# Attention and dense experts in one block: slots written out, rows split, turned and routed tile by tile, first dense products among attention's last steps

## The chip, the cores and the metric

The kernel runs on one core of a Trainium2 chip. The metric is the device time of one execution in microseconds (us); the median of several runs counts. The core has TensorE (PE, matmuls and transposes), VectorE (DVE), ScalarE (ACT), GpSimd (POOL) and SyncE (SP, which issues most of the transfers). Each engine works through its own instructions in order and waits on semaphores for the others.

## What is computed

The input x has 2048 rows of 256 numbers (16 tiles of 128 rows). Two layers follow each other, each with a residual: an attention with fp8-rounded projections, half of it over the rows themselves and half over a second input `ctx`, and a feed-forward layer with a shared (dense) expert and a choice of 2 out of 8 experts for each row. Cut to its core:

```python
x = x + xattn(layernorm(x), ctx)          # q, k, v, qx by fp8-rounded products; kx, vx from ctx; wproj
h = layernorm(x)
logits = h @ router_w
top_logits, top_indices = top_k(logits, 2);  scores = softmax(top_logits)
combined = sum over the 2 experts e chosen: score * ((silu(h @ w1[e][:, :512]) * (h @ w1[e][:, 512:])) @ w2[e])
shared = (silu(h @ w_gate) * (h @ w_up)) @ w_down          # 1024 wide
x = x + combined + shared
```

## The kernel before

**Three blocks of instructions.** The program has three blocks, one after the other, and at a block's end all engines wait for each other: attention; the dense expert with the routing; the eight experts. The change is about the first two.

**Attention.** Its work is cut into 64 units: for each of the 16 tiles i four units r (0 and 1 over the rows themselves, 2 and 3 over ctx). `run_slots` lays the steps of the units out in slots: in slot N every engine does one step each of several units, and the number beside a step says how far ahead of N its unit is. On TensorE a slot holds, in this order, the scores of unit N+1 (`pe_scores`), the first transposes of N+2, project 0 of N+3, the turn of the probabilities of N (`pe_probT`), project 1 of N+3, the second transposes of N+2 (`pe_transpose(1)`), the values of N-1 (`pe_values`), project 2 of N+3, the third transposes of N+2, the output product of N-2 (`pe_out`) and project 3 of N+3. VectorE's slot begins with the maximum of the scores of N+1 (`mx`) and the first scaling `nrm` of N+2, which the second transposes read. Slots -3 to 7 and 44 to 66 are written out; slots 8 to 43 are a loop (`Fori`) over tiles, with the tile's number in a register. ScalarE also squares the 30 pieces of the feed-forward weights (`act_weight_squares`, one in every second slot), whose sums give the scales by which the weights are split into two fp16 halves.

**Dense block.** Before its first product it must have the sums of all 30 pieces, six small steps on VectorE that turn them into scales (`scales_end`), the layer norm of the rows (`rstd3`, `normalise`), each row split into two fp16 numbers (`rows_high` on ScalarE, `rows_low` on VectorE), transposed in pairs of tiles (`turn`), evicted (`turned`) and multiplied by the router's weights (`route`), and the pieces 0 to 3 of the dense weights loaded and split (`shared`). Then 32 slots follow (`run_slots3`): 4 groups of 512 rows by 8 slices of 128 of the 1024 columns. In slot N TensorE does `up` of N+1, which is a gate product and an up product of 6 matmuls each, and `down` of N-1 (12 matmuls); ScalarE does silu of the gate (`gate`), one weight piece, and the high half of the product; VectorE does the product (`product`), one weight piece and the low half. Gate and up have two banks each, so the pair of N+1 waits until the product of N-1 has been read. The choice of experts, its sorting and the positions of the rows are done on VectorE in slots 4 to 14, and GpSimd scatters the rows into `xbuf` in memory.

Of the kernel before, what the change touches and what calls it, by code (L numbers as in the profile page):

```python
# [5 lines left out]
F32 = mybir.dt.float32  # L6
# [59 lines left out]
def build(nc, x, ctxT, cols, w_all, wprojT,  # L66
# [4 lines left out]
    with ExitStack() as top:  # L71
        def sb(name, shape, dt, stack=top):
            return stack.enter_context(nc.sbuf_tensor(name, shape, dt))
# [16 lines left out]
        wsum = sb("wsum", [P, NPC + 1], F32)  # L90
        rw = sb("rw", [P, KT, E], F32)
        st3 = sb("st3", [P, NT, 6], F32)
        mv3 = sb("mv3", [P, NT, 2], F32)
        ve3 = sb("ve3", [P, NT], F32)
        rs3 = sb("rs3", [P, NT], F32)
        EARLY = 12

        def moments(dve, tiles):
            for t in tiles:
                dve.bn_aggr(mv3[:, t, :], st3[:, t, :]).then_inc(s["mv3_done"], 1)  # L100

        def rstd3(pool, n, tiles):

            a, b = tiles.start, tiles.stop
            pool.wait_ge(s["mv3_done"], b)
            pool.tensor_scalar(ve3[:, a:b], mv3[:, a:b, 1], EPS, None, ALU.add).then_inc(s["ve3"], 1)
            pool.wait_ge(s["ve3"], n + 1)
            pool.tensor_tensor(rs3[:, a:b], ve3[:, a:b], neghalf[:, a:b], ALU.pow).then_inc(s["rs3"], 1)

# [3 lines left out]
        RING = 13  # L113
        xq_all = sb("xq", [P, RING, KT, 4, P], F16, attn)
        w_hi = sb("w_hi", [P, KT, NG * BANK], F16, attn)
        w_lo = sb("w_lo", [P, KT, NG * BANK], F16, attn)
        ctxh = sb("ctxh", [P, NT, KT, P], F16, attn)
        ctxl = sb("ctxl", [P, NT, KT, P], F16, attn)
# [18 lines left out]
                 "wsq_done wtot_done nst_in wst_in2 x ln_step mv_done rstd_done x_in0 x_in1 x_in2 x_in3 n3_pool rw16_done rwsq_done").split()  # L137
# [16 lines left out]

        with ExitStack() as ph:
            cmat = sb("cmat", [P, P], F32, ph)
            ones = sb("ones", [P, P], F32, ph)
# [18 lines left out]
            sqsum = sb("sqsum", [P, 5], F32, ph)  # L176
            csum = sb("csum", [P, 2], F32, ph)
            half2, shift2, root2, npow, ninv, nsc = (sb(n, [P, 2], F32, ph)
# [19 lines left out]
            zero = sb("zero", [P, ROW], F16, ph)  # L198
            nst = sb("nst", [P, PIECE], F32, ph)
            rwsq = sb("rwsq", [P, KT * E], F32, ph)  # L200
            b_pj = [bank(f"b_pj{n}", ph) for n in range(2)]
            b_tr = bank("b_tr", ph)
            b_pt = bank("b_pt", ph)
            b_sc = bank("b_sc", ph)
            b_o = [bank(f"b_o{n}", ph) for n in range(2)]
            b_acc = bank("b_acc", ph)
# [4 lines left out]
            def xq_place(a, n):  # L211
                return xq_all[:, a:a + n, :, :, :].rearrange("p a k j t -> p (a k j t)")

            def ring(t):
                return bass.ds(t % RING if isinstance(t, int) else t, 1)

            w16 = [rows16(catq[:, n, :, :].rearrange("p a b -> p (a b)")) for n in range(2)]
            w16 += [rows16(xq_place(2 + n, 1)) for n in range(2)]
            w32 = [rows16(xq_place(4 + 2 * n, 2).bitcast(F32)) for n in range(4)]
# [15 lines left out]
            block = ph.enter_context(nc.Block())  # L235

            ORDER = ((0, 1, 2, 3), (0, 1, 2, 3), (1, 2, 0, 3), (1, 2, 0, 3))
            PARTS = (JK, JQ, JV, JQX)
            PREP = 7

# [27 lines left out]
            def run_slots(eng, steps, between, behind):  # L268

                def slot(i, r):  # L270
                    for ahead, step, *label in steps:
                        ui, ur = i + (r + ahead) // 4, (r + ahead) % 4
                        if not isinstance(ui, int) or (1 if ahead == PREP else 0) <= ui < NT:
                            step(eng, ui, ur)
                        if label and isinstance(i, int):
                            behind.get((4 * i + r, label[0]), lambda: None)()
# [1494 lines left out]
```

## Time and profile before

| | us |
|---|---|
| median of 3 runs | 1041.06 (1040.61 to 1041.09) |
| profiled execution, its own time | 1039.99 |
| its span, first to last instruction | 1038.2 |
| TensorE busy | 958.3 (92%) |
| attention, from the first instruction to the last of its residuals | 0 to about 675 |
| dense block | about 675 to 826 |
| experts | 826 to 1038.2 |

The span is what the profile accounts for. "Busy" is time in which an instruction of the engine was under way; TensorE's matmuls overlap, so the step between the starts of two of its rows, not the length of one, is what a matmul costs.

### The profile page before, as it was taken

The page shows a single profiled execution, that of the slowest core. Times are in us where ns is not written, and L with a number is a line of the kernel's source. Part 1 is how long each engine was busy: PE and PEld are TensorE (multiplying, and loading weights), DVE is VectorE, ACT ScalarE, POOL GpSimd, SP SyncE. Part 2 cuts the span into 40 slices and gives each one's busy share as a digit, 9 for nine tenths or more (in the row PEclk, how much of TensorE's full clock was granted, in tenths as well). Part 3 has the DMA queues.
Part 4 walks back from the last instruction along what each step waited for, and adds up shares of the span by engine and source line. Part 5 has one row for each costly group of instructions (what it writes and reads, how often), then busy time and mean ns, then how long its engine had stood idle before and what let it go on. Part 6 is the DMA issues. An engine that isn't in the chain of part 4 may idle for free. (4 is left out here: it accounts for less than half of the span.)

```text
span 1038.2 us, 23492 instructions
## 1 busy us (share of the span) xinstructions
PE 958.3 (92%) x7238; PEld 678.3 (65%) x7239; DVE 796.6 (77%) x1694; ACT 737.7 (71%) x1348; POOL 437.7 (42%) x642
## 2 busy tenths in 40 slices
PE   5488999999999999999999999759999799999995
PEld 3356777777777777777777777635566456666663
DVE  7678999999999999999999999766887534444441
ACT  6778888888888888888878887366465444544552
POOL 5225554545554455445444545270255012233222
PEclk9799999999999999999999999969999999999997
DMA  9922310010010100100101001041366364222222
GB/s 270 249 67 42 61 42 22 21 40 20 21 40 20 40 20 20 40 20 20 42 22 41 22 22 42 1 164 48 98 206 199 129 167 88 25 25 28 28 25 25
DMA packets 32697, 65.51 MB, mean 63 GB/s; under 512 B 3712, under 2 KB 20736, under 8 KB 32512
## 3 DMA queue, kind: packets, MB, share of 16 engines
q1 hardware_dynamic: 23184, 50.20, 15.4%
q0 software_dynamic: 9456, 14.59, 8.3%
q8 instruction: 32, 0.52, 0.2%
q14 instruction: 25, 0.20, 0.1%
HBM read 53.42 MB, written 16.59 MB: 67 GB/s over the span
## 5 line engine op out<-in xcount | busy, mean ns | idle before, releaser
L605 POOL TENSOR_TENSOR root<-vareps,neghalf 128x4 f32<-128x4 f32 (+1 forms) x128 | 173.7, 1357 | 10.0
L598 POOL TENSOR_TENSOR var<-ssq,unit 128x4 f32<-128x4 f32 (+1 forms) x128 | 53.1, 415 | 275.1 <-DVE ssq L465 275.1
L337 PE MATMUL b_pj<-w_hi,xq 128*128 128x512 f16 x384 | 147.7, 385 | 2.1 <-DVE xq L588 1.5
L337 PE MATMUL b_pj<-w_lo,xq 128*128 128x512 f16 x384 | 147.0, 383 | 0.0
L409 ACT ACTIVATE sq<-b_pj 128x512 f32<-128x512 f32 x192 | 114.1, 594 | 45.9 <-PE b_pj L337 44.8
L465 DVE TENSOR_REDUCE ssq<-sq 128x4 f32<-128x512 f32 x192 | 129.9, 677 | 9.8 <-ACT sq L409 9.7
L1548 POOL DMA_INDIRECT out<-xg x39 | 60.6, 1554 | 168.8 <-ACT xg L1650 156.9
L476 DVE TENSOR_TENSOR nrm<-raw,rstd 128x512 f32<-128x512 f32 x192 | 128.1, 668 | 4.6 <-POOL rstd L609 3.8
L363 PEld LDWEIGHTS b_sc<-kT,qT 128*128 128x128 f32 x1024 | 123.1, 192 | 7.2 <-ACT qT L435 0.3
L353 PE MATMUL b_tr<-ident,nrm 128*128 128x128 f32 x768 | 116.9, 275 | 5.9 <-DVE nrm L476 5.4
L363 PE MATMUL b_sc<-kT,qT 128*128 128x64 f32 x1024 | 121.5, 272 | 0.0
L419 ACT ACTIVATE raw<-b_pj 128x512 f32<-128x512 f32 x192 | 115.6, 602 | 0.0
L353 PEld LDWEIGHTS b_tr<-ident,nrm 128*128 128x128 f32 x768 | 93.7, 146 | 32.2 <-DVE nrm L476 8.3
L435 ACT ACTIVATE qT<-b_tr,col 128x512 f32<-128x512 f32 x128 | 99.6, 778 | 4.2 <-PE b_tr L353 4.2
L1688 DVE SCALAR_TENSOR_TENSOR ea<-b_eu,uu,esg 128x512 f32<-128x512 f32 x39 | 29.3, 751 | 88.2 <-ACT esg L1635 88.2
L514 DVE TENSOR_TENSOR cat<-b_o,rsm 128x512 bf16<-128x512 f32 x128 | 81.9, 680 | 2.3 <-PE b_o L386 2.3
L1635 ACT ACTIVATE esg<-b_eg,ug 128x512 f32<-128x512 f32 x39 | 26.8, 688 | 74.4 <-PE b_eu L1569 74.4
L386 PE MATMUL b_o<-probT,v 64*128 64x128 f32 x1024 | 75.3, 287 | 0.0
L386 PEld LDWEIGHTS b_o<-probT,v 64*128 64x128 f32 x1024 | 63.0, 189 | 10.8 <-issue 10.8
L435 ACT ACTIVATE kT<-b_tr,col 128x512 f32<-128x512 f32 x64 | 49.5, 774 | 28.8 <-PE b_tr L353 28.8
L398 PE MATMUL b_acc<-wproj,catq 128*128 128x256 f16 x512 | 66.9, 274 | 1.3 <-DVE catq L529 1.3
L337 PEld LDWEIGHTS b_pj<-w_hi,xq 128*128 (+1 forms) x384 | 37.7, 98 | 33.4 <-DVE xq L588 1.8
(290 smaller groups left out, 2291.4 us busy)
## 6 DMA issues: line engine op xcount, KB each, us to landing
nst<-in_ffw SPq DMA_DIRECT2D x30, 512.0 KB, 3.2
wload<-in_ffw SPq DMA_DIRECT2D x30, 512.0 KB, 3.8
xbuf<-zero SPq DMA_DIRECT2D x39, 129.0 KB, 5.4
xg<-xbuf SPq DMA_DIRECT2D x9, 516.0 KB, 3.8
x_sb<-in_x SPq DMA_DIRECT2D x4, 512.0 KB, 11.4
wproj<-in_ctxT SPq DMA_DIRECT2D x1, 2048.0 KB, 8.1
xq<-in_w_all SPq DMA_DIRECT2D x4, 512.0 KB, 19.8
wproj<-in_wprojT POOLq DMA_DIRECT2D x4, 512.0 KB, 5.3
```

What stands on the lines that cost most here:

```text
L337: last = pe.matmul(o, x, w[:, k, at:at + BANK], start=(k == 0 and n_ == 0), stop=(k == KT - 1 and n_ == len(terms) - 1))
L353: last = pe.transpose(o, nrm[:, c, hd * P:(hd + 1) * P], ident[:, :])
L363: last = pe.matmul(b_sc[:, (g * 2 + b) * S:(g * 2 + b + 1) * S], qT[:, r % 2, g * 2 + b, :], kT[:, r % 2, g, b * S:(b + 1) * S], start=Tru ...
L386: last = pe.matmul(b_o[b][:, g * P:(g + 1) * P], v[b * S:(b + 1) * S, r, g, :], probT[b * S:(b + 1) * S, r % 2, g, :], start=True, stop=True)
L398: last = pe.matmul(b_acc[:, 0:H], catq[:, r % 2, hd, :], wproj[:, r * n + hd, :], start=(r == 0 and hd == 0), stop=(r == 3 and hd == n - 1))
L409: act.activation(sq[:, (r * NN + c) % 2, :], b_pj[c % 2][:, :], ACT.Square).then_inc(s["sq_done"], 1)
L419: act.activation(raw[:, r % 2, c, :], bk, ACT.Copy).then_inc(s["raw_done"], 1)
L435: act.activation(flat(dst), b_tr[:, :], ACT.Identity, scale=col[:, at:at + 1], bias=col[:, at + 1:at + 2]).then_inc(s["tev_done"], 1)
L465: dve.tensor_reduce(ssq[:, r % 2, c, :], sq[:, (r * NN + c) % 2, :].rearrange("p (a b) -> p a b", b=D), axis=AX.X, op=ALU.add).then_inc(s[ ...
L476: dve.tensor_tensor(nrm[:, c, :].rearrange("p (a b) -> p a b", b=D), raw[:, r % 2, c, :].rearrange("p (a b) -> p a b", b=D), wide(rstd[:, ...
L514: last = dve.tensor_tensor(cat16[:, :, b * S:(b + 1) * S], b_o[b][:, :].rearrange("p (a b) -> p a b", b=S), wide(rsm[:, r * n:(r + 1) * n] ...
L605: pool.tensor_tensor(root[:, r % 2, c, :], vareps[:, r % 2, c, :], neghalf[:, 0:1].unsqueeze(2).to_broadcast(shape), ALU.pow).then_inc(s[" ...
```

## The change

**One block.** The dense block's body is joined to attention's. Both have their own instruction order per engine, and a dictionary `tail` puts dense work behind named steps of attention's last slots. `run_slots` now writes out all slots, -3 to 67. The dense products reuse attention's PSUM banks.

**Rows tile by tile.** For each tile t, VectorE takes the statistics one slot earlier and `bn_aggr` in slot 4t+5, GpSimd does epsilon, power and the normalised tile `n3` there, ScalarE and VectorE the two halves `xr` in slot 4t+6, TensorE the four transposes (`pe_rows`) at the end of slot 4t+7, into the bank `b_pt` of the probabilities, and ScalarE the eviction; `pe_route(t)` stands in slot 4t+10. Each split tile is stored to memory (`rowbuf`), and all come back as `xn` in one transfer of 2 MB in the dense part.

**Scales in two parts.** The router's sum goes with the context's at the start. The sums of the six dense pieces are taken in slots 56 to 58, those of the experts' pieces in slot 66. The squares start two slots earlier.

**Dense products 0 to 6 among attention's last slots.** FIRST is 62: gate and up n go into slot 61 + n; down 0 into slot 65, 1 and 2 into 66, 3 and 4 into 67. `run_slots3` goes on from slot JOIN = 6. The routing steps on VectorE are put three slots later (7 to 17), and the scatter of a row tile waits for four more dense slots. The gate and up weights are laid out in halves of 512 columns, so that pieces 0 and 1 are enough for the first four slices. The expert block is the same; its first four tiles `xg0` now lie in the place of `xl`, so that their load waits for the last up product.

```diff
             def run_slots(eng, steps, between, behind):
-                slots(-3, 8)
-                if 8 in between:
-                    between[8]()
-                with eng.Fori(2, RING - 2) as i:
-                    for r in range(4):
-                        slot(i, r)
-                slots(4 * (RING - 2), 4 * NT + 3)
+                for N in range(-3, 4 * NT + 4):
+                    if N in between:
+                        between[N]()
...
+            def pe_rows(pe, t, part):
+                if part != 2:
+                    return
+                pe.wait_ge(s["xn_done"], t + 1)
+                after(pe, "xh_done", t)
+                after(pe, "ptev_done", min(4 * t + 8, 4 * NT) if isinstance(t, int) else 4 * t + 8)
+                for a in range(2):
+                    for k in range(KT):
+                        last = pe.transpose(b_t[:, a, k, :], xr[:, a * H + k * P:a * H + (k + 1) * P], ident16[:, :])
+                last.then_inc(s["t3_done"], 1)
...
+            def act_rows(act, t, part):
+                if part == 1:
+                    act.wait_ge(s["n3_pool"], t + 1)
+                    after(act, "t3_done", t)
+                    after(act, "row_out", 16 * t)
+                    act.activation(xr[:, 0:H], n3, ACT.Copy, scale=XS).then_inc(s["xnh_done"], 1)
+                if part == 2:
+                    act.wait_ge(s["t3_done"], t + 1)
+                    act.activation(xhl[:, :, :, bass.ts(t, P)], b_t[:, :, :, :], ACT.Copy).then_inc(s["xh_done"], 1)
...
+            def dve_rows(dve, t, part):
+                if part == 0:
+                    dve.wait_ge(s["st3_done"], t + 1)
+                    after(dve, "n3_pool", t)
+                    dve.bn_aggr(mv3[:, :], st3[:, :]).then_inc(s["mv3_done"], 1)
+                if part == 1:
+                    dve.wait_ge(s["xnh_done"], t + 1)
+                    dve.scalar_tensor_tensor(xr[:, H:2 * H], n3, XS, xr[:, 0:H], ALU.mult, ALU.subtract)\
+                        .then_inc(s["xn_done"], 1)
...
+            def pool_rows(pool, t, part):
...
+                pool.wait_ge(s["mv3_done"], t + 1)
+                pool.tensor_tensor(ve3[:, :], mv3[:, 1:2], epsc[:, 0:1], ALU.add).then_inc(s["ve3"], 1)
+                pool.wait_ge(s["ve3"], t + 1)
+                pool.tensor_tensor(rs3[:, :], ve3[:, :], neghalf[:, 0:1], ALU.pow).then_inc(s["rs3"], 1)
+                pool.wait_ge(s["rs3"], t + 1)
+                pool.tensor_scalar(n3, x_sb[:, t, :], mv3[:, 0:1], rs3[:, 0:1], ALU.subtract, ALU.mult).then_inc(s["n3_pool"], 1)
...
-                    (-3, dve_stats),
+                    (-2, dve_stats),
                     (-1, dve_round),
                     (PREP, dve_quantize, "tokens"),
+                    (ROWS, dve_rows, "rows"),
...
             def _(sp):
+                attention_sync(sp)
+                sp.wait_ge(s["proj_done"], 4 * (4 * NT - 2))
                 for n in range(NPC):
+                    if n == 2:
+                        sp.wait_ge(s["wsq_done"], NPC)
                     after(sp, "wl_done", n - 2)
                     sp.dma_start(stage[n % 3][:, :], ffw[n, :, :]).then_inc(s[f"wst_in{n % 3}"], 16)
+                    if n == 4:
+                        store_rows(sp, NT - 2)
+                    if n == 6:
+                        store_rows(sp, NT - 1)
+                        sp.wait_ge(s["row_out"], 16 * NT)
+                        sp.wait_ge(s["proj_done"], 16 * NT)
+                        sp.dma_start(xn[:, :, 0:2 * H].bitcast(U32), rowbuf).then_inc(s["rows_in"], 16)
...
+                def first_gate(n):
+                    def run():
+                        if n == 0:
+                            pe.wait_ge(s["xh_done"], 4)
+                            pe.wait_ge(s["raw_done"], 16 * NT)
+                        if n == 1:
+                            pe.wait_ge(s["tev_done"], NN * 4 * NT)
+                        pe.wait_ge(s["wl_done"], 2 if n < 4 else 4)
+                        after(pe, "a_done", n - 1)
+                        up_part(0, 0, n)
+                    return run
...
+                for n in range(JOIN + 1):
+                    tail[FIRST - 1 + n, "project 0"] = first_gate(n)
+                    tail[FIRST - 1 + n, "project 1"] = first_up(n)
+                tail[FIRST + 3, "project 3"] = downs(0)
+                tail[FIRST + 4, "first transposes"] = expert_sums
+                tail[FIRST + 4, "project 3"] = downs(1, 2)
+                tail[FIRST + 5, "project 3"] = downs(3, 4)
```

**How the order moves.** The next two fences show TensorE from the start of slot 61. Before, the engine has attention's steps alone there (`b_sc` scores, `b_tr` transposes, `b_pt` probabilities, `b_o` values, `b_acc` output):

```order
L363 MATMUL b_sc<-kT,qT 128x64 x8
L353 MATMUL b_tr<-ident,nrm 128x128 x4
L376 MATMUL b_pt<-ident,prob 128x128 x4
L353 MATMUL b_tr<-ident,nrm 128x2x64 x4
L386 MATMUL b_o<-probT,v 128x128 x8
L353 MATMUL b_tr<-ident,nrm 128x2x64 x4
L398 MATMUL b_acc<-wproj,catq 128x256 x8
L363 MATMUL b_sc<-kT,qT 128x64 x8
L376 MATMUL b_pt<-ident,prob 128x128 x4
```

With the change, TensorE from the start of slot 61:

```order
L355 MATMUL b_sc<-kT,qT 128x64 x8
L345 MATMUL b_tr<-ident,nrm 128x128 x4
L1219 MATMUL b_pj<-xhl,gateh 128x512 x2
L1219 MATMUL b_pj<-xhl,gatel 128x512
L1219 MATMUL b_pj<-xhl,gateh 128x512 x2
L1219 MATMUL b_pj<-xhl,gatel 128x512
L372 MATMUL b_pt<-ident,prob 128x128 x4
L1219 MATMUL b_pj<-xhl,uph 128x512 x2
L1219 MATMUL b_pj<-xhl,upl 128x512
L1219 MATMUL b_pj<-xhl,uph 128x512 x2
L1219 MATMUL b_pj<-xhl,upl 128x512
L345 MATMUL b_tr<-ident,nrm 128x2x64 x4
```

A gate product of six matmuls now stands behind the first transposes and an up product behind the probabilities, where the projections of later units stood in the slots before; slots 62 to 67 follow the same pattern.

The next two fences show VectorE at the border of slots 57 and 58, before and with the change (`catq` is attention's output on its way to the fp8 rounding, `x_sb` the residual, `st` and `mv` statistics, `mx` the maximum and `nrm` the scaling that TensorE's second transposes wait for). Before:

```order
L523 TENSOR_SCALAR catq<-cat 128x1024
L536 SCALAR_TENSOR_TENSOR x_sb<-b_acc,cout,x_sb 128x256
L529 TENSOR_SCALAR catq<-catq 128x1024
L485 TENSOR_REDUCE mx<-b_sc 128x8
L476 TENSOR_TENSOR nrm<-raw,rstd 128x512
```

With the change:

```order
L567 SCALAR_TENSOR_TENSOR x_sb<-b_acc,cout,x_sb 128x256
L574 BN_STATS st<-x_sb 128x6
L560 TENSOR_SCALAR catq<-catq 128x1024
L580 BN_AGGR mv<-st 128x2
L618 TENSOR_SCALAR whalf<-b_pt 128x3
L620 TENSOR_SCALAR wshift<-whalf 128x3
L623 TENSOR_SCALAR wroot<-wshift 128x3
L626 TENSOR_SCALAR upow<-wroot 128x3
L628 RECIPROCAL ainv<-upow 128x3
L630 TENSOR_SCALAR wsc<-ainv 128x3
L931 TENSOR_SCALAR us<-upow 128x1
L932 TENSOR_SCALAR us<-ainv 128x1
```

Two more steps on `us` follow, and only then `mx` and `nrm`. The statistics and the `BN_AGGR` stand there for every tile, the ten small steps of the scales in this slot alone.

The last fence shows TensorE's order at slot 63 with the change, where a dense pair stands beside attention's shrunken slot (`xr` is the split tile 14):

```order
L1219 MATMUL b_pj<-xhl,gateh 128x512 x2
L1219 MATMUL b_pj<-xhl,gatel 128x512
L372 MATMUL b_pt<-ident,prob 128x128 x4
L1219 MATMUL b_pj<-xhl,uph 128x512 x2
L1219 MATMUL b_pj<-xhl,upl 128x512
L382 MATMUL b_o<-probT,v 128x128 x8
L419 MATMUL b_acc<-wproj,catq 128x256 x8
L394 MATMUL b_pt<-ident,xr 128x128 x4
```

Between the values `b_o` and the next gate product only the output product and, here, four transposes are left.

## Rows read from the trace of the kernel before

**Rows 1.** Windows, busy us per engine (instructions), granted clock: slot 22 (loop), slot 58 (written out).

```profile
281.11:290.12 9.01, 9.01 (x74) 6.92 (x73) 8.31 (x19) 8.87 (x19) 4.32 (x9) 1.00 0.16 58
622.79:631.79 9.00, 9.00 (x73) 6.93 (x72) 8.58 (x18) 7.92 (x15) 4.68 (x9) 1.00 0.16 60
```

**Rows 2.** Timeline of TensorE in slot 22: start, us, instruction.

```profile
281.11 1.90 PE L363 MATMUL b_sc<-kT,qT 128*128 128x64 f32 x16
282.84 0.61 PE L353 MATMUL b_tr<-ident,nrm 128*128 128x128 f32 x4
283.29 0.38 PE L337 MATMUL b_pj<-w_hi,xq 128*128 128x512 f16 x1
...
285.45 0.60 PE L353 MATMUL b_tr<-ident,nrm 128*128 128x128 f32 x4
285.98 1.16 PE L386 MATMUL b_o<-probT,v 64*128 64x128 f32 x16
287.07 0.39 PE L337 MATMUL b_pj<-w_hi,xq 128*128 128x512 f16 x1
```

**Rows 3.** Windows: slot 61 to first dense product, to dense slot 6, to the end.

```profile
651.54:688.58 37.04, 21.14 (x195) 17.28 (x194) 28.25 (x62) 15.58 (x23) 17.28 (x15) 0.78 0.21 73
688.58:721.19 32.61, 31.25 (x241) 18.23 (x242) 20.20 (x77) 21.60 (x29) 7.78 (x9) 0.93 0.24 80
721.19:824.14 102.95, 101.01 (x630) 61.32 (x627) 79.03 (x140) 56.81 (x76) 36.45 (x34) 1.00 0.48 149
```

**Rows 4.** Timeline of TensorE between the blocks, in brackets idle before and releaser.

```profile
676.13 0.58 PE L1195 MATMUL b_m<-wjob,w2l 128*128 128x20 f32 x2 [2.12 <-DVE wjob L1287]
...
688.58 1.03 PE L1165 MATMUL b_g<-xhl,gateh 128*128 128x512 f16 x2 [3.18 <-DVE upl L1081]
```

**Rows 5.** Timeline of TensorE in the dense block: turn, route, up and down.

```profile
693.34 0.61 PE L1135 MATMUL b_t<-ident,xn 128*128 128x128 f16 x8
693.79 0.59 PE L1165 MATMUL b_g<-xhl,gateh 128*128 128x512 f16 x2
...
696.54 0.21 PE L1145 MATMUL b_m<-rw,xhl 128*128 128x16 f16 x2
...
696.75 0.61 PE L1135 MATMUL b_t<-ident,xn 128*128 128x128 f16 x8
...
717.29 0.59 PE L1165 MATMUL b_g<-xhl,gateh 128*128 128x512 f16 x2
...
719.88 0.27 PE L1179 MATMUL b_y<-downh,ah 128*128 128x256 f16 x1
...
721.19 0.59 PE L1165 MATMUL b_g<-xhl,gateh 128*128 128x512 f16 x2
```

**Rows 6.** Timeline of VectorE in slot 22.

```profile
283.52 0.23 DVE L584 TENSOR_SCALAR xq<-y 128x256 bf16 x1 [0.66 <-ACT y L570]
...
284.53 0.68 DVE L476 TENSOR_TENSOR nrm<-raw,rstd 128x512 f32<-128x512 f32 x1
```

**Rows 7.** Timeline of VectorE: four aggregates; `cat`; a dense product.

```profile
675.90 0.37 DVE L100 BATCH_NORM_AGGREGATE mv<-st 128x2 f32<-128x6 f32 x4
...
656.66 1.28 DVE L514 TENSOR_TENSOR cat<-b_o,rsm 128x512 bf16<-128x512 f32 x2
...
700.48 0.75 DVE L1445 SCALAR_TENSOR_TENSOR a<-b_u,us,sg 128x512 f32<-128x512 f32 x1
```

**Rows 8.** Timeline of GpSimd: normalised tiles beside a working and an idle VectorE.

```profile
683.70 7.32 POOL L1087 TENSOR_SCALAR w1h<-x_sb,mv,rs 128x256 f32<-128x256 f32 x4
691.01 2.42 POOL L1087 TENSOR_SCALAR w2h<-x_sb,mv,rs 128x256 f32<-128x256 f32 x2
```

**Rows 9.** Window of VectorE with the ten small steps of the context's scale.

```profile
47.48:49.05 1.57, 1.36 (x10) 0.63 0.74 209
```

**Rows 10.** Timeline of ScalarE: the router weights' squares.

```profile
666.53 0.21 ACT L741 ACTIVATE rwsq<-rw 128x16 f32<-128x16 f32 x1
```

**Rows 11.** DMA issues: KB each, median us from issue to landing.

```profile
out<-x_sb SPq DMA_DIRECT2D x1, 2048.0 KB, 8.1
```

More of the change, by code:

```diff
@@ L102, in rstd3 @@
[L102 to L108, printed above, removed]
+        st3 = sb("st3", [P, 6], F32)
+        mv3 = sb("mv3", [P, 2], F32)
+        ve3 = sb("ve3", [P, 1], F32)
+        rs3 = sb("rs3", [P, 1], F32)
@@ L1153, in ranks, with up_part @@
                     pe.matmul(b_rank, before, both.rearrange("p a b -> p (a b)"), start=True, stop=True)
-                    pe.matmul(b_tot, ones, both.rearrange("p a b -> p (a b)"), start=True, stop=True)\
+                    pe.matmul(b_tot, ones[:, :], both.rearrange("p a b -> p (a b)"), start=True, stop=True)\
                         .then_inc(s["rank_done"], 1)
+                def up_part(c, g, f):
+                    n = NF * g + f
+                    w, b = ((sw[0], b_g), (sw[1], b_u))[c]
+                    for k in range(KT):
+                        for m, (part, xx) in enumerate(((0, xh), (0, xl), (1, xh))):
+                            last = pe.matmul(b[f % 2][:, :], w[part][:, k * SF + f * P:k * SF + (f + 1) * P],
+                                             xx[:, k, g * BANK:(g + 1) * BANK],
+                                             start=(k == 0 and m == 0), stop=(k == KT - 1 and m == 2))
+                    if c:
+                        last.then_inc(s["gu_done"], 1)
                 def up(pe, g, f):
@@ L1473, in _, with counts_and_scans @@
-                rows_low(1)
-                shared(0)
-                shared(1)
-                shared(2)
-                shared(3)
-                rows_low(2)
-                rows_low(3)
-                units()
+                def counts_and_scans():
+                    counts()
+                    tile_scans()
+                tail = {(FIRST - 2, "token norm"): shared(0), (FIRST - 2, "squares 2"): shared(1),
+                        (FIRST + 2, "tokens"): expert_scales}
+                for n in range(JOIN):
+                    if n:
+                        tail[FIRST + n, "token norm"] = lambda n=n: low(dve, 0, n - 1)
+                    tail[FIRST + n, "norm 0"] = lambda n=n: product(dve, 0, n)
@@ L1485, in _ @@
-                    (2, "product"): in_order((rows_low, 7)),
-                    (4, "weights"): choose, (5, "weights"): indices, (6, "weights"): marks,
-                    (7, "weights"): in_order((scores,), (counts,)), (8, "weights"): tile_scans,
-                    (9, "weights"): expert_scans, (10, "weights"): rows, (11, "weights"): tiles,
-                    (12, "weights"): codes, (13, "weights"): expert_units, (14, "weights"): expert_units_end,
+                    (7, "weights"): choose, (8, "weights"): indices, (9, "weights"): marks,
@@ L1490, in _ @@
+                    (10, "weights"): scores, (11, "weights"): counts_and_scans,
+                    (12, "weights"): expert_scans, (13, "weights"): rows, (14, "weights"): tiles,
+                    (15, "weights"): codes, (16, "weights"): expert_units, (17, "weights"): expert_units_end,
                 })
-        normed.close()
+        banks.close()
         with ExitStack() as ph:
```

504 lines of the change are left out of this document (232 added, 272 removed).

## The prediction

> **What bounds the kernel now.** I read the windows first: in attention's steady slots TensorE is busy for all of the time, at full clock (9.01 of 9.01 us in slot 22, where VectorE has 8.31 and ScalarE 8.87) [rows 1]. Slot 22 lies in the loop and slot 58 in the part that is written out before as well; both take 9.0 us, so writing the slots out is worth nothing by itself. There a microsecond saved elsewhere buys nothing, and every TensorE step added costs its length. Then the windows around the border of the blocks [rows 3]. From the start of slot 61 to the first dense product 37.04 us pass with 21.14 busy at a mean clock of 0.78; the next 32.61 us, to the start of dense slot 6, run at 0.93; the last 102.95 have 101.01 busy at 1.00. The timeline names the waits: the sums wait for VectorE, the first dense product waits 3.18 us for a split weight piece [rows 4]. So the loss lies between 651.54 and 721.19, and here the change works.
>
> **The steps.** At full clock a step is the distance between two starts. In slot 22: scores 1.73 us, four fp32 transposes 0.45 (0.53 for the second ones), values 1.09 [rows 2]. In the dense block: eight fp16 transposes 0.45, the routing of two tiles 0.21, a gate and up pair of 12 matmuls 2.59, `down` 1.31 [rows 5]. `down` has 12 matmuls of 256 columns, so attention's output product with 8 of them is 0.87.
>
> **1. The border: minus 26.0.** The same TensorE work in both: scores 2 x 1.73, transposes 0.45 + 0.53 + 0.45, probabilities 3 x 0.45, values 4 x 1.09, output products 5 x 0.87, seven pairs 7 x 2.59, five `down` 5 x 1.31, and of the row work two turns and one routing, with the sum about 0.65. Together 40.3 us, against 69.65 from 651.54 to 721.19. What waits remain? Gate, up and product have two sets of banks, so pair n+2 waits for product n. In slots 62 to 64 VectorE does `cat` first, which waits for TensorE's values, then the product: 1.28 + 0.75 = 2.03 [rows 7]. TensorE has only the output product (0.87) between values and the next gate, in slot 63 also a turn (0.22). That leaves waits of 1.2, 0.9 and 1.2, sum 3.3. From slot 65 `cat` is gone and two `down` cover the product. So 43.6 in place of 69.65. The bounds of the waits are 0 (the order of VectorE hides them) and 8.4 (1.2 for each of seven pairs). In rows 4 a wait of 2.12 us stands just ahead of the loss of clock; these are shorter, so I leave the clock at full.
>
> **2. Row work moved into attention: plus 4.5.** Fourteen tiles are turned before slot 61 (14 x 0.225) and thirteen routed (13 x 0.105) [rows 5], in slots where nothing hides them. The same work is gone from the 69.65, so this is a move and no added work.
>
> **3. Lateness in each tile: plus 1.4.** In slot 22 `nrm` starts at 284.53 and lasts 0.68, to 285.21; the second transposes start at 285.45 [rows 6, 2]. So 0.24 us of room, of which some 0.08 is the way from one engine to the other. With the change `BN_AGGR` stands ahead (0.37 for four, 0.09 each [rows 7]); the statistics ahead of it fall into the 0.66 us that VectorE waits for ScalarE [rows 6]. GpSimd's `n3` of 256 columns now runs beside VectorE in just this slot. In the rows it is GpSimd that pays: four take 7.32 us beside a working VectorE, 1.83 each, two take 2.42 beside an idle one, 1.21 each [rows 8]. I give VectorE 0.15 for it: 0.09 + 0.15 - 0.16 is about 0.1, times 14. The bounds are 0 and the whole 1.21 (rival A). GpSimd itself has room, busy 4.32 of 9.01 [rows 1]. ScalarE has little, 8.87 of 9.01, and gets a copy of 256 columns at the end of this slot and an eviction of 512 at the end of the next; I take it that the lighter slots beside absorb both, and the bound for that is inside rival A's.
>
> The Trainium skill speaks against this (SBUF — State Buffer, section "SBUF: two separate sides"): the port pair that VectorE and GpSimd share is an exclusive lock, held for a whole instruction, also against a VectorE operation with two SBUF inputs, which `nrm` is. Rows 8 agree in that GpSimd is held up. By the page `nrm` could be held for the whole `n3`, which is rival A; no row before has `n3` beside `nrm`.
>
> **4. The scales in slot 58: plus 0.7.** Ten small steps now stand ahead of `mx` and `nrm` in slot 58. Ten such steps took 1.57 us [rows 9]; the chain has one link more in sequence, so 1.8. The token's norm and rounding are no longer there this late, worth about 0.9 (0.66 of waiting and two short steps [rows 6], less the statistics), and 0.16 of room: 0.7 us of wait for the second transposes. Bounds 0 and 1.8.
>
> **5. Start: plus 0.3.** The router's squares (0.21 and a read of the sum [rows 10]) go into the chain ScalarE, VectorE, TensorE of the context's scale, for which TensorE waits. The staging in other tiles and the earlier squares fall into ScalarE's idle time.
>
> **6. After slot 6: minus 0.9.** 25 pairs and 27 `down` are 64.8 + 35.4 = 100.2; with the last routing 0.2, the ranks 0.5 and the wait before the last `down` of 1.1 that is 102.0, against 102.95 [rows 3]. The wait for the marks of the choice goes, since they are ready a slot earlier than they are needed.
>
> **7. Transfers: plus 0.5.** SP, which works in order, stores the last row tile (slot 66), waits, fetches all rows (2 MB) and only then piece 7 of the weights, which ScalarE needs in slot 7. 2 MB took 8.1 us to landing [rows 11]. From the split of tile 15 I count store 2.5, fetch 8.1, piece about 2: landing 13 to 14 us later, where ScalarE asks for it after 10, and its high half is late for `down` after another 4. It just fits; the bounds are 0 and 3. At the end of the block the scatter ends one pair before the last and the load of `xg0` follows the last up product; both then land about when VectorE's last outputs do, bounds 0 and 1. I take 0.5 for both.
>
> The sum: -26.0 + 4.5 + 1.4 + 0.7 + 0.3 - 0.9 + 0.5 = -19.5. It is made against the span of 1038.2, to which the profiled execution adds 1.8 outside (1039.99); its time lies 1.07 under the median of 1041.06. The part outside does not change, so I subtract from the median: **1021.6 us**.
>
> **The rivals.**
>
> A. VectorE is held for each `n3`. Speaks for it: both engines touch the same tiles in the same 2 us, and the room is 0.16. Against it: in the rows GpSimd is the one that waits. Price: 1.21 + 0.09 - 0.16 = 1.14 in each of 14 tiles, 16.0 in place of 1.4: 1036.2.
>
> B. The other side: as A, but each `n3` holds `nrm` for the 1.83 us that it takes beside a working VectorE. The place is the second transposes of every slot 4t+6, the price 1.83 + 0.09 - 0.16 = 1.76, times 14 is 24.6 in place of 1.4: 1044.8, slower. It decides from 1.5 us for each tile on, (19.5 + 1.4) / 14. Against it: the same as for A, and GpSimd's own length there is made of waiting.
>
> C. More waits at the border: every one of the seven pairs waits 1.2 for its banks (ScalarE's table load before the first silu stands in this chain too), 8.4 in place of 3.3: 1026.7.
>
> D. Piece 7 is late by 3 us and `xg0` by 1: 4 in place of 0.5: 1025.1.
>
> E. VectorE and the transfers keep up everywhere: no waits in 1, 3, 4 and 7, 5.9 less: 1015.7.
>
> F. The dense products do not overlap at all, because the split pieces 0 and 1 or the scales come too late for slot 61, and the old gap stays; the 4.5 us of row work are then in attention and not in the gap: 1041, no change. Against it: pieces are loaded from slot 59 on and split in slot 60, ahead of slot 61 by about 1 us.
>
> **How the numbers follow.** The forecast has 0.56, C 0.14, D 0.10, E 0.09, A 0.05, B 0.04, F 0.02. Forecast, C and D and most of E lie between 1015.5 and 1030; A, B, F and worse mixtures are left out, some 0.15. A, C, D, E and the forecast are faster: 0.94; F is the same: 0.02; B is slower: 0.04. A measurement of this kernel can tell about 0.2%, 2 us, from no change.
>
> **What would show it.** Windows: slot 22 goes from 9.01 us to about 9.2 and slot 23 gains 0.22; more than 10 in slot 22 speaks for A or B, and then the second transposes' wait for `nrm` stands first among TensorE's waits. TensorE's first dense product stands before attention's last scores; from slot 61 to dense slot 6 about 44 us at a clock near 1.00; the waits there are of gate products for VectorE's `a`, about 1 us each, three of them. One wait of 0.7 for `nrm` in slot 58. From slot 6 to the end of the block about 102 us; a wait of `down` 7 there is D. Wrong would be the forecast if the clock falls among the mixed slots, since each microsecond at half clock costs half, or if the waits repeat in each tile.

## The result, and the profile after

| | before | after |
|---|---|---|
| median, us | 1041.07 (4 runs) | 1024.38 (4 runs, 1024.13 to 1025.15) |
| ratio, 95% interval | | 0.9843 (0.9831 to 0.9855) |
| span of the profiled execution | 1038.2 | 1022.0 |

The kernel is 16.7 us faster by the medians and 16.2 by the spans, and the interval of the ratio lies clear of 1. The forecast was 1021.6 us, 19.5 less than before, so 3 us have to be found. The windows of the changed kernel answer to [rows 1] and [rows 3]: slot 22, slot 23, slot 58, slot 61 to dense slot 6, dense slot 6 to the end of the block. Each row has the stretch, its length, the busy time of TensorE, of its weight loads, of VectorE, ScalarE and GpSimd with the numbers of instructions, the granted clock, and the DMA engines' share and GB/s.

```profile
282.74:291.85 9.11, 9.11 (x78) 7.04 (x77) 8.83 (x20) 8.96 (x19) 6.34 (x11) 1.00 0.21 58
291.85:301.95 10.10, 10.10 (x81) 7.44 (x80) 9.74 (x21) 8.02 (x17) 5.46 (x10) 1.00 0.04 15
627.96:637.59 9.63, 9.41 (x80) 6.97 (x78) 9.39 (x28) 7.89 (x15) 6.02 (x11) 1.00 0.20 57
657.61:702.14 44.53, 41.31 (x315) 28.13 (x314) 33.14 (x65) 19.45 (x29) 9.40 (x13) 1.00 0.19 58
702.14:807.50 105.36, 101.69 (x642) 61.55 (x639) 84.71 (x192) 60.56 (x81) 39.69 (x34) 1.00 0.55 174
```

The border shrank from 69.65 us to 44.53. TensorE's idle time there fell from 17.3 us to 3.2 and its busy time from 52.39 to 41.31. Two things lowered the busy time: the clock is now 1.00 throughout, and most of the turns and routings are no longer in this stretch (about 4.6 us at full clock). The last row is the surprise: 105.36 us against 102.95 before [rows 3], where 102.0 was forecast. VectorE has more to do in it, 84.71 against 79.03, but its busy share is no reason by itself; the waits are. In the views below `a` is a dense product on VectorE, `al` its low half, which `down` needs, and `sg` the silu of the gate on ScalarE. Waits of TensorE from 657 to 808 (us in total, times, longest):

```profile
PE b_o L1264 <- DVE al L1467: 3.7, 4, 1.2
PE b_pj L1219 <- DVE a L1474: 2.3, 2, 1.2
PE b_tr L1219 <- DVE a L1474: 0.9, 1, 0.9
```

The three waits for `a` are the forecast ones. Of the four for `al` (the `down` products) one stood before too, ahead of the last `down`; the other three are new. TensorE's timeline at the three gates, each with the step ahead of it:

```profile
672.25 1.03 PE L419 MATMUL b_acc<-wproj,catq 128*128 128x256 f16 x8
674.41 0.59 PE L1219 MATMUL b_pj<-xhl,gateh 128*128 128x512 f16 x2 [1.12 <-DVE a L1474]
...
679.51 0.39 PE L394 MATMUL b_pt<-ident,xr 128*128 128x128 f16 x4
680.83 0.59 PE L1219 MATMUL b_tr<-xhl,gateh 128*128 128x512 f16 x2 [0.94 <-DVE a L1474]
...
684.61 1.05 PE L419 MATMUL b_acc<-wproj,catq 128*128 128x256 f16 x8
686.81 0.59 PE L1219 MATMUL b_pj<-xhl,gateh 128*128 128x512 f16 x2 [1.16 <-DVE a L1474]
```

In brackets stands 1.12, 0.94, 1.16, together 3.2. By the distance of the starts it is more: 2.16 from the output product to the gate, where the product is worth 0.87, so 1.29, then 1.09 and 1.33, together 3.7. A wait costs about 0.16 us more than its bracket. The bracket counts from the modelled end of the row ahead, and that row is longer than its step: the output product's is 1.03 long with a step of 0.87.

### The profile page after: what moved, and what is told of

Same layout as the page of the kernel before. It is cut to its first block and busy times, and to the rows that moved or that the text cites. A ratio compares the mean times of both kernels' runs of the same rounds, so it can differ in the third digit from the quotient of the medians.

```text
span 1022.0 us, 22255 instructions
## 1 busy us (share of the span) xinstructions
PE 955.7 (94%) x7240; PEld 677.0 (66%) x7241; DVE 797.4 (78%) x1704; ACT 735.2 (72%) x1364; POOL 452.4 (44%) x673
## 3 DMA queue, kind: packets, MB, share of 16 engines
q1 hardware_dynamic: 27552, 54.39, 17.3%
## 5 line engine op out<-in xcount | busy, mean ns | idle before, releaser
L1567 POOL DMA_INDIRECT out<-xg x35 | 54.3, 1551 | 114.9 <-ACT xg L1669 90.8
L329 PEld LDWEIGHTS b_pj<-w_hi,xq 128*128 128x128 f16 x384 | 37.7, 98 | 33.1 <-DVE xq L647 1.8
```

The costliest lines, as they stand in the source:

```text
L329: last = pe.matmul(o, x, w[kind][:, k, at:at + BANK], start=(k == 0 and n_ == 0), stop=(k == KT - 1 and n_ == len(terms) - 1))
```

## The experiments

All edits are to the changed kernel. The profiles differ where nothing was edited: slot 58 starts at 627.6 to 629.5 us. Nearly all of this arises ahead of slot 1, for from slot 1 to slot 58 each of them takes 550.0. The expert block varies by 1 us. The stretches between hardly vary: in the second profile of the changed kernel they came back within 0.06 us. So small effects are read from three stretches: slot 58, the border (start of slot 61 to the first gate of dense slot 6, behind the turn that stands at its head) and the dense rest (from there to the first expert transpose).

| kernel | median, us | ratio to before (interval) | slot 58 | border | dense rest |
|---|---|---|---|---|---|
| changed kernel | 1024.38 | 0.9843 (0.9831 to 0.9855) | 9.63 | 44.76 | 107.07 |
| the same again | 1024.65 | 0.9846 (0.9833 to 0.9860) | 9.64 | 44.76 | 107.01 |
| products ahead of `cat` | 1022.26 | 0.9827 (0.9814 to 0.9841) | 9.65 | 41.87 | 107.44 |
| rows fetched late | 1023.37 | 0.9838 (0.9824 to 0.9851) | 9.64 | 44.76 | 105.11 |
| units a slot later | 1023.40 | 0.9838 (0.9824 to 0.9851) | 9.64 | 44.76 | 105.60 |
| scales split | 1024.10 | 0.9845 (0.9832 to 0.9858) | 9.20 | 44.76 | 107.15 |
| `n3` twice | 1026.38 | 0.9862 (0.9847 to 0.9877) | 9.63 | 44.75 | 109.54 |
| no overlap | 1032.10 | 0.9917 (0.9904 to 0.9931) | 9.63 | 55.00 | 104.40 |
| half the overlap | 1026.00 | 0.9858 (0.9843 to 0.9873) | 9.63 | 49.40 | 104.41 |
| no overlap, late pieces | 1042.45 | 1.0019 (1.0009 to 1.0030) | 9.63 | 65.20 | 104.41 |
| four edits together | 1018.39 | 0.9788 (0.9775 to 0.9801) | 9.19 | 41.86 | 104.00 |

The first four edits change the whole by less than their intervals can part from the changed kernel; there the verdict rests on the stretches.

**The changed kernel again.** 

> The changed kernel once more, beside the next three on the same chip, so that they can be compared with it and not only with the kernel before. All stretches from slot 58 on should be those of its first profile within 0.05 us (slot 58 9.63, slot 61 to dense slot 6 44.76 to the first gate of slot 6, from there to the expert block 107.07); the stretch ahead of slot 58 and the expert block may differ by about a microsecond, as they did between the first four experiments, where nothing had been changed in them.

The three stretches came back as 9.64, 44.76 and 107.01, so they can be compared between kernels.

**Products ahead of `cat`.** 

> VectorE does the gate products 0 to 2 of slots 62 to 64 ahead of attention's `cat` instead of behind it; nothing else changes. In the changed kernel three gates wait 1.12, 0.94 and 1.16 us for `a`, and VectorE itself stands idle 1.22, 0.94 and 1.45 us ahead of the same `cat` steps. My theory (the gate waits only because the product is queued behind `cat`, which waits for TensorE's values): the three waits go, 3.2 us less, 1021.2 us. Rival 1 (the product would not be ready to run earlier, since ScalarE's `sg` comes late): no change, 1024.4. Rival 2 (the wait only moves: `cat` and with it the output product come later by the 0.75 us of a product): half of it or less is won, 1022.5 to 1023.5.

```diff
-                    tail[FIRST + n, "norm 0"] = lambda n=n: product(dve, 0, n)
+                    tail[FIRST + n, "squares 1" if n < 3 else "norm 0"] = lambda n=n: product(dve, 0, n)
```

The border fell by 2.89 us, less than the 3.7 of the waits, and the median of 1022.26 lies above the theory's 1021.2. All three waits for `a` are gone, as the theory says. One new wait of 0.48 stands in slot 63, where the probabilities wait for VectorE's `prob`. VectorE's timeline in slot 62 of this kernel shows why:

```profile
672.81 0.75 DVE L1474 SCALAR_TENSOR_TENSOR a<-b_pj,us,sg 128x512 f32<-128x512 f32 x1 [1.32 <-ACT sg L1306]
673.48 1.28 DVE L545 TENSOR_TENSOR cat<-b_o,rsm 128x512 bf16<-128x512 f32 x2
674.67 0.19 DVE L532 RECIPROCAL rc<-sm 128x8 f32<-128x8 f32 x1
674.90 0.69 DVE L536 TENSOR_TENSOR prob<-prob,rc 128x512 f32<-128x512 f32 x1
```

The first product waits 1.32 us for `sg`, in front of which ScalarE loads silu's table, so it can't run much earlier (rival 1), and it now delays `cat` and what follows (rival 2), here `prob`. Behind the other two products no wait is left. The dense rest grew by 0.37: a border that is shorter by 2.9 us meets weight piece 7 at the same time, and `down` 7 waits 0.93 in place of 0.58.

**Rows fetched late.** 

> SP stores the last row tile and fetches all rows (2 MB) behind weight pieces 7 and 8 instead of ahead of them. In the changed kernel ScalarE waits 2.22 us for piece 7, VectorE 1.92 us behind it, and then two `down` wait 0.58 and 0.81 us for `al`. Theory (these two waits come from the late piece, which leaves VectorE's sorting steps no room): piece 7 is there when asked for, both waits go or shrink to 0.3 together, 1.1 to 1.4 us less, about 1023.1. Rival 1 (the first wait is the late piece, the second one comes from VectorE's own load of sorting steps and outputs in slots 8 and 9): 0.6 less, 1023.8. Rival 2 (VectorE is full in slots 7 to 9 whatever the piece does): no change, 1024.4.

```diff
-                    if n == 6:
+                    if n == 8:
                         store_rows(sp, NT - 1)
                         sp.wait_ge(s["row_out"], 16 * NT)
```

First the changed kernel. The DMA queue of SP issues the fetch of `xn`, then pieces 7 and 8; ScalarE waits for piece 7 (2.22), and VectorE for ScalarE (1.92); in VectorE's order the low half of the piece (L1156) and then sorting steps, among them the maxima (L1366), stand ahead of `al` 7:

```profile
697.86 0.63 SPq L1174 DMA_DIRECT2D xn<-rowbuf  x1
698.53 2.70 SPq L1167 DMA_DIRECT2D wload<-in_ffw  x1
```

```profile
708.61 1.15 ACT L1151 ACTIVATE w1h<-wload,wsc 128x1024 f16<-128x1024 f32 x1 [2.22 <-DMA wload<-in_ffw]
```

```profile
709.80 1.28 DVE L1156 SCALAR_TENSOR_TENSOR w1l<-wload,wsc,w1h 128x1024 f16<-128x1024 f32 x1 [1.92 <-ACT w1h L1151]
...
711.64 1.19 DVE L1366 MAX8 w2h<-w2l 128x8 f32<-128x8 f32 x16
...
712.97 0.68 DVE L1467 SCALAR_TENSOR_TENSOR al<-a,ah 128x512 f16<-128x512 f32 x1
...
717.85 0.68 DVE L1467 SCALAR_TENSOR_TENSOR al<-a,ah 128x512 f16<-128x512 f32 x1
```

Piece 7 landed 10.06 us after its issue, at 708.59. With the fetch behind piece 8 SP issues piece 7 at 689.58 instead of 698.53, it lands 3.70 us later, and ScalarE splits it without a wait:

```profile
689.58 0.33 SPq L1167 DMA_DIRECT2D wload<-in_ffw  x1
```

```profile
707.02 1.15 ACT L1151 ACTIVATE w1h<-wload,wsc 128x1024 f16<-128x1024 f32 x1
```

The waits of 0.58 and 0.81 both go and the third falls from 1.16 to 0.94: 1.96 us, more than the theory had. The late piece was the cause of both; rivals 1 and 2 fall.

**Units a slot later.** 

> The two last routing steps on VectorE (the experts' units, 1.9 us and some 0.6 us) go from dense slots 16 and 17 to 17 and 18. In the changed kernel `down` waits 1.16 us for `al` at 751.56, right behind these steps and the outputs of slot 17. Theory (routing steps and outputs meet because all routing was put three slots later): VectorE gets a light slot between and the wait goes: 0.9 to 1.2 us less, 1023.3. Rival (VectorE has no room after slot 17 either, and the wait comes one slot later): no change, 1024.4.

```diff
-                    (15, "weights"): codes, (16, "weights"): expert_units, (17, "weights"): expert_units_end,
+                    (15, "weights"): codes, (17, "weights"): expert_units, (18, "weights"): expert_units_end,
```

In the changed kernel VectorE does the units' four steps (L1449 to L1452, 1.7 us until the outputs start), the outputs and only then `al`:

```profile
747.79 0.51 DVE L1449 TENSOR_TENSOR w1h<-ehot,upow 128x312 f32<-128x312 f32 x1
...
749.51 1.40 DVE L1486 SCALAR_TENSOR_TENSOR x_sb<-b_o,us,x_sb 128x512 f32<-128x512 f32 x2
750.82 0.68 DVE L1467 SCALAR_TENSOR_TENSOR al<-a,ah 128x512 f16<-128x512 f32 x1
```

With the units one slot later the wait is gone and none comes behind it: 1.47 us less in the dense rest. Of this 1.16 is the wait, 0.16 what a wait costs beyond its bracket, and 0.14 a shorter wait of `down` 7 (0.44).

**Scales split.** 

> In slot 58 only the first of the ten small scale steps (the read of the sums) stays ahead of `mx` and `nrm`; the other nine go behind the last `nrm` of the slot. Slot 58 takes 9.63 us in the changed kernel against 9.11 in the other slots of its kind. Theory (the second transposes wait for `nrm` behind these steps): slot 58 comes down to 9.1 to 9.2, 0.45 to 0.5 us less, about 1023.9. Rival (something later in the slot, as the exponentials or the squares, comes late instead, since VectorE is nearly full): 0 to 0.2 less.

```diff
-                    (SHARED_SLOT - 1, "tokens"): shared_scales, (SHARED_SLOT + 1, "token norm"): shared_scales_end,
+                    (SHARED_SLOT - 1, "tokens"): shared_scales, (SHARED_SLOT + 1, "token norm"): shared_sums_read,
+                    (SHARED_SLOT + 1, "squares 0"): shared_scales_end,
```

Here `shared_sums_read` does the first step of the chain, the read of the bank. Slot 58 took 9.20 us, 0.43 less; the wait for `nrm` is gone. The median says nothing on so little.

**`n3` twice.** 

> GpSimd computes each tile's `n3` twice, the second time over the first with the same values, before it reports. In the changed kernel one takes 1.23 us in all 16 tiles, beside VectorE's `prob` and `nrm`, which take 0.68 each as they did before. Theory (in these slots neither engine holds up the other): again 1.23 each, VectorE's steps beside it unchanged at 0.68, and the second transposes do not wait; the only price is that GpSimd's next step, the `rstd` of the next unit, comes 0.5 us later where VectorE has room, 0 to 0.3 per tile, 0 to 4 us in all. Rival (the shared port is held for a whole instruction): VectorE's steps beside it stretch or start late by 1.2 us per tile, 17 us more.

```diff
+                pool.tensor_scalar(n3, x_sb[:, t, :], mv3[:, 0:1], rs3[:, 0:1], ALU.subtract, ALU.mult).then_inc(s["ve3b"], 1)
+                pool.wait_ge(s["ve3b"], t + 1)
                 pool.tensor_scalar(n3, x_sb[:, t, :], mv3[:, 0:1], rs3[:, 0:1], ALU.subtract, ALU.mult).then_inc(s["n3_pool"], 1)
```

GpSimd and VectorE in slot 22 of this kernel:

```profile
285.90 1.23 POOL L684 TENSOR_SCALAR zero<-x_sb,mv,rs 128x256 f32<-128x256 f32 x1
287.23 1.22 POOL L686 TENSOR_SCALAR zero<-x_sb,mv,rs 128x256 f32<-128x256 f32 x1
```

```profile
285.93 0.68 DVE L523 TENSOR_TENSOR prob<-b_sc,mx 128x512 f32<-128x512 f32 x1
286.53 0.68 DVE L507 TENSOR_TENSOR nrm<-raw,rstd 128x512 f32<-128x512 f32 x1
287.13 0.68 DVE L496 TENSOR_REDUCE ssq<-sq 128x4 f32<-128x512 f32 x1
```

`prob` lies wholly and the `nrm` behind it almost wholly (all but 0.08 us) beside a running `n3`; `nrm` takes 0.68 us, as it did without one [rows 6], and starts 0.60 behind its neighbour as ever. In the changed kernel itself the second `nrm` of each such slot lies beside `n3` for 0.60 us or more in 14 of the 16 tiles, and it is 0.68 long in each. The steady slots did not grow, so a second `n3` costs nothing in attention. The dense rest lost 2.5 us, by `down` 7, which now waits 3.27: piece 7 lands 2.7 us later against slot 61 than in the changed kernel. For 1.3 of this the last tile is ready later, and with it the fetch; the other 1.4 is a slower landing of the piece (11.42 us after its issue), whose cause is open. It is the mechanism of the fetch experiment from the other side.

**No overlap.** 

> Everything of the change stays but the overlap: no dense product stands among attention's steps, pair 0 follows the last slot's projection steps, and dense slots 0 to 5 run behind attention as before. Row work in the tiles, early scales and early weight pieces remain. Theory (most of the 25 us won at the border come from filling TensorE's idle time and so holding its clock; attention's last slots alone leave it idle for some 7 of 24.6 us, with clock dips): from slot 61 to dense slot 6 50 to 60 us in place of 44.76, the mean clock there below 1, 1024 + 5 to 15, middle 1034. Rival (the overlap is worth nearly nothing, the gain is that rows, scales and pieces are ready when attention ends): 46 us or less there, 1024 to 1026. Other rival (the overlap is everything): the old 69, about 1049.

**Half the overlap.** 

> Half of the overlap: gate and up products 0 to 3 stand in slots 64 to 67 of attention, down 0 and 1 in slot 67, dense slots go on from 3. Everything else is the changed kernel. With all seven pairs the stretch from slot 61 to the first gate of dense slot 6 takes 44.76 us, with one pair behind the last slot 55.00. Theory (each slot filled saves what TensorE would have waited in it, and the light slots 61 to 63 are where VectorE's chain is longest and the clock dips first): 49 to 52 us. Rival (the gain lies in slots 65 to 67, which hold almost no attention work of TensorE's own): 45 to 46 us.

JOIN is 0 or 3 in place of 6, and the pairs stand in the last slots:

```diff
-            JOIN = 4 * NT + 4 - FIRST
+            JOIN = 0
+            TAIL = 4 * NT + 4 - JOIN
...
-                    tail[FIRST - 1 + n, "project 0"] = first_gate(n)
-                    tail[FIRST - 1 + n, "project 1"] = first_up(n)
-                tail[FIRST + 3, "project 3"] = downs(0)
+                    tail[TAIL - 1 + n, "project 0"] = first_gate(n)
+                    tail[TAIL - 1 + n, "project 1"] = first_up(n)
```

The border takes 55.00 us without overlap and 49.40 with half of it: 10.2 us for all pairs, 4.6 for the pairs of slots 61 to 63, so the light slots carry nearly half. The theory's 49 to 52 held; the rival, which put the gain into slots 65 to 67, had 45 to 46. The window of the border without overlap and TensorE's waits in it:

```profile
657.29:712.29 55.00, 46.59 (x320) 30.69 (x318) 35.35 (x67) 22.36 (x33) 8.90 (x13) 0.91 0.29 91
```

```profile
PE b_pt L372 <- DVE prob L536: 2.4, 1, 2.4
PE b_acc L419 <- DVE catq L560: 2.0, 1, 2.0
PE b_tr L345 <- DVE nrm L507: 1.7, 1, 1.7
```

Half of the 10.2 us is idle time (8.4 in place of 3.2). The other half is busy time, 46.59 in place of 41.31 for the same work and one turn more, at a mean clock of 0.91. Some of it comes back: the dense rest is 2.6 us shorter, and ScalarE no longer waits for piece 7, which landed at 700.29, well ahead of dense slot 6. Net 7.5 us by the medians beside each other, 1032.10 against 1024.65, within the theory's 5 to 15.

**No overlap, late pieces.** 

> As the kernel without overlap, whose stretch from slot 61 to the first gate of dense slot 6 takes 55.00 us, but the six weight pieces of the dense part are split late: 0 and 1 in slots 66 and 67, 2 and 3 behind dense slot 0, 4 and 5 behind dense slot 1 (the store of row tile 14 stands before they are waited for). So it shows how much of the 14.65 us by which 55.00 is less than the 69.65 of the kernel before comes from pieces that are ready early, as against rows and scales. Theory (pieces and rows each carry a part, since before ScalarE and VectorE did both behind attention): first gates wait for the pieces, 58 to 63 us. Rival 1 (the pieces fit into gaps anyway, rows and scales were the whole of it): 55 to 56. Rival 2 (pieces were the whole of it): 66 or more.

```diff
-                tail = {(FIRST - 3, "tokens"): shared(0), (FIRST - 2, "raw 1"): shared(1), (FIRST - 1, "raw 3"): units_known}
+                tail = {(FIRST + 4, "tokens"): shared(0), (FIRST + 5, "tokens"): shared(1), (FIRST - 1, "raw 3"): units_known}
```

VectorE's parts move likewise. The window and the two longest waits:

```profile
658.29:723.49 65.20, 47.13 (x319) 29.83 (x318) 35.90 (x66) 23.96 (x34) 7.29 (x12) 0.87 0.25 85
```

```profile
PE b_pj L1220 <- DVE upl L1157: 6.0, 1, 6.0
PE b_o L1269 <- issue: 5.7, 1, 5.7
```

65.20 us, 10.2 above the kernel without overlap: TensorE's first product waits 6.0 for the split `upl`, the first `down` 5.7, by the order of the program for piece 4. The theory had 58 to 63 and missed; rival 2 had 66 or more. The number is not the price of late pieces alone. In ScalarE's order piece 1 (`uph`) now stands behind the high half of the last row tile, for which it waits 6.67 us:

```profile
683.35 0.42 ACT L479 ACTIVATE xr<-zero 128x256 f16<-128x256 f32 x1 [6.67 <-POOL zero L684]
683.68 1.13 ACT L1152 ACTIVATE uph<-wload,wsc 128x1024 f16<-128x1024 f32 x1
```

So the first wait is one for a row tile as much as for a piece, and another place for the late pieces would give another number. It is no exact copy of before.

**Four edits together.** 

> The four edits together: products ahead of `cat` in slots 62 to 64, the fetch of all rows behind weight pieces 7 and 8, the experts' units one slot later, the nine scale steps behind the last `nrm` of slot 58. By the stretches that each one showed alone: slot 58 9.20 in place of 9.63 (0.43 less), slot 61 to the first gate of slot 6 41.9 in place of 44.76 (2.9 less), from there to the expert block 107.07 less the three waits for `al` of 0.58, 0.81 and 1.16 us (2.55) and no more than 0.5 of new ones: 104.3 to 104.8. Together 5.6 to 5.9 us less than the changed kernel, about 1018.4. If the savings of the pieces and of the earlier products hide each other, 4 us less.

```profile
628.25:637.44 9.19, 9.19 (x80) 7.11 (x78) 8.98 (x26) 7.88 (x15) 6.88 (x10) 1.00 0.19 60
657.47:699.11 41.64, 41.15 (x316) 28.11 (x315) 33.20 (x65) 19.23 (x29) 9.40 (x13) 1.00 0.28 83
699.11:801.40 102.29, 101.17 (x642) 61.78 (x639) 84.63 (x192) 60.70 (x81) 42.98 (x34) 1.00 0.55 170
```

1018.39 us, 6.3 less than the changed kernel beside it on the same chip and a ratio of 0.9788 to the kernel before. The edits add up (0.45 + 2.9 + 3.0 in the stretches), and of all the waits from slot 58 to the end of the block only the 0.5 for `prob` and the old 1.1 ahead of the last `down` are left.

## Why the prediction came out as it did

| step | forecast | measured | from |
|---|---|---|---|
| 1 border | -26.0 | -25.1 | 69.65 to 44.53 |
| 2 row work | +4.5 | +5.4 | 14 x 0.23, 13 x 0.10, 14 x 0.06 |
| 3 lateness | +1.4 | 0 | second transposes where they were |
| 4 slot 58 | +0.7 | +0.5 | 9.63 against 9.11 |
| 5 start | +0.3 | +0.2 | slot 1 at 77.97, was 77.76; varies by 2 |
| 6, 7 dense rest | -0.4 | +2.4 | 102.95 to 105.36 |
| experts | 0 | +0.4 | 214.5 against 214.06, varies by 1 |
| sum | -19.5 | -16.2 | spans |

**Right: the border.** The waits came where they were put (slots 62, 63 and 64) and at 1.12, 0.94, 1.16 for 1.2, 0.9, 1.2, and the cause that was given, the product queued behind `cat`, is shown by moving it. The clock stayed at 1.00. It took 0.9 us more than I gave it: the waits are 3.7 by step distances, 0.4 over the forecast, and gaps of some 0.1 ahead of values, scores and up products come to 0.7. Against this, one turn (0.23) stands in dense slot 6 and not in the border, where I had counted it.

**Right in sum by luck, wrong in mechanism: 2 and 3.** The two have 5.9 in the forecast and 5.4 measured. I gave 1.4 to lateness at the second transposes. There is none: they start 4.34 us into slot 22, before [rows 2] and after. The 0.10 by which that slot grew is the routing of one tile, which falls into this same slot and costs 0.11. What I had not counted is 0.06 in the slot behind each turn, where the step from the scores to the transposes is 1.79 us in place of 1.73. VectorE and GpSimd in slot 22 of the changed kernel:

```profile
284.87 0.23 DVE L643 TENSOR_SCALAR xq<-y 128x256 f16<-128x256 bf16 x1 [0.21 <-ACT y L612]
...
285.27 0.17 DVE L580 BATCH_NORM_AGGREGATE mv<-st 128x2 f32<-128x6 f32 x1
285.36 0.66 DVE L516 TENSOR_REDUCE mx<-b_sc 128x8 f32<-128x512 f32 x1
285.94 0.68 DVE L507 TENSOR_TENSOR nrm<-raw,rstd 128x512 f32<-128x512 f32 x1
```

```profile
286.51 1.23 POOL L684 TENSOR_SCALAR zero<-x_sb,mv,rs 128x256 f32<-128x256 f32 x1
```

`nrm` starts 3.20 us into the slot, before it was 3.42 [rows 6]. (The view names the tile `n3` by its place, `zero`.) `xq` comes earlier by 0.28 because its `y` does, and that pays for `BN_AGGR`. And `n3` cannot hold up this `nrm`: it starts 0.57 behind it, after the two short GpSimd steps. I had put both into "the same 2 us" without laying out GpSimd's chain.

**Rivals A and B** fall by this order, and by the experiment with two `n3` for the later `nrm` too. The Trainium skill's exclusive lock of the port pair for a whole instruction (SBUF — State Buffer, section "SBUF: two separate sides") is not what this pair shows: neither `n3` at 1.23 us nor `nrm` at 0.68 is any longer beside the other. Before, the normalised tiles took 1.83 each beside VectorE's splitting of weight pieces [rows 8]. That is a mean: the four took 1.22, 1.51, 3.06 and 1.58. Nor was GpSimd the only one to pay, as the forecast had it: VectorE's split beside the first took 1.50 us where the next two took 1.28. What makes that pair different was not tried.

**4** was 0.7 and is 0.5, the mechanism is shown by the split. The bracket of the wait for `nrm` is only 0.2. **5** can't be judged: slot 1 starts at 77.37 to 79.50 us in the profiles of the changed kernel and its variants, against one profile before.

**Wrong: 6 and 7.** Step 6 said that 25 pairs, 27 `down` and the old wait are all, 102.0; it set the routing steps, moved three slots later, at nothing. Step 7 let piece 7 "just fit". The runs show both failed, and together. The landing itself was counted well: 12.5 us behind the split of tile 15 for 13 to 14, and ScalarE asked for it after 10.3, for 10. The step that failed is the slack behind it. I counted until `down` needs the weights; but the two `down` wait for `al`, which stands in VectorE's order behind the low half of the late piece. Piece 7 came 2.22 us after ScalarE asked for it, the mechanism of rival D, and VectorE, with sorting steps in slots 7 and 8 and outputs in 9, could not catch up. It cost two waits of 1.4 together by their brackets, and 2.0 by the fetch experiment. Three slots later the units met the outputs of slot 17, another 1.16 us (1.5 by the experiment), which no rival had. Without the late piece, or with the units elsewhere, these waits go. 105.36 less the three waits (2.55, and 0.16 more for each) and one turn (0.23) is 102.1, against 102.0.

**The other rivals.** By the number alone the result lies nearer to D (1025.1) than to the forecast (1021.6); D's mechanism was there, at 2.0 us where D had 3 for the piece. C and E are excluded (three waits for `a`, no more and no fewer), F by the border. F's price was also added up wrongly: with its own terms it comes to 1043 and not 1041.

**Where the gain is from.** I wrote the border as work and waits, as if overlap were its cause. Undone in steps it goes 44.8, 55.0 without overlap, 65.2 with late pieces too, 69.65 before. So the overlap gives 10.2 us of it, 7.5 by the medians of the whole. The rest, 14.65, is what was made ready early: pieces, rows and scales, and the 4.6 of turns and routings that step 2 says were only moved. How the other 10 divide between pieces and rows stays open, since in the kernel with late pieces the first product's wait hangs on both.

## What to carry to other kernels

When two phases are joined, ask for each product moved forward what its consumer engine does just ahead of it: three orders of steps on VectorE and one of transfers on SP left 6 us here, which four small edits took back. Put bulk transfers that are not needed yet behind the small ones that the next phase needs at once, and when a chain of small steps is moved by some slots, lay it beside the periodic work (outputs, weight pieces) of the slots that it lands in. A gain with several parts is best undone part by part: the overlap, which the change is named for, was less than half of the gain at the border.

## What the hardware showed unexpectedly

A switch of ScalarE between exp and silu cost 1.28 us, and nothing beside it shows: the activations follow within 0.03 us. Both ways, in dense slot 8:

```profile
714.99 1.28 ACT L1300 ACT_TABLE_LOAD   x1
716.29 0.31 ACT L1300 ACTIVATE egap<-gap,us 128x16 f32<-128x16 f32 x1
716.61 1.28 ACT L1306 ACT_TABLE_LOAD   x1
```

The granted clock stayed at 1.00 through waits of 1.1 us in slots 62 to 64 with TensorE busy for 41.31 of 44.53 us. Without overlap it averaged 0.91, and there a gate and up pair started at 683.52 took 5.1 us in place of 2.59. Ahead of it stood waits of 0.67, 2.01 and 0.78 us within 7 us:

```profile
681.27 1.05 PE L419 MATMUL b_acc<-wproj,catq 128*128 128x256 f16 x8 [2.01 <-DVE catq L560]
683.10 0.58 PE L1284 MATMUL b_acc<-wjob,ones 128*128 128x16 f32 x2 [0.78 <-DVE x_sb L567]
683.52 1.01 PE L1220 MATMUL b_pj<-xhl,gateh 128*128 128x512 f16 x2
```

A single wait is no sign by itself: behind the one of 2.37 us for `prob` in the same kernel the steps kept their full-clock lengths (values 1.09).

`n3` on GpSimd took 1.23 us in every tile beside attention's VectorE work, and from 1.22 to 3.06 us beside the splitting of weight pieces.
